# Making the second attention's keys and values during routing, and splitting them at the end of the experts

## The chip, the cores and the metric

One core of a Trainium2 chip runs the kernel; the metric is the device time of one execution in microseconds (us), the median of several. The core has five engines with a queue each: TensorE (PE in the profile; PEld is its weight load), VectorE (DVE), ScalarE (ACT), GpSimd (POOL) and SyncE (SP, which here only issues transfers; GpSimd issues the gathers). They meet at semaphores: an instruction adds to one, and another queue waits until it has a value.

## The reference

Two transformer-like layers over 2048 tokens of 256 numbers (`x`, 2 x 1024 x 256), all in fp32:

```python
x = x + tanh(g_xattn[0]) * L0_xattn(layernorm(x), ctx)   # 16 heads of 64, 154 keys per batch
x = x + tanh(g_ffn[0])   * L0_ffn(layernorm(x))          # 8 experts, top 2, silu(a) * g, width 512
x = x + tanh(g_xattn[1]) * L1_xattn(layernorm(x), ctx)   # 8 heads of 128, all 308 keys together
x = x + tanh(g_ffn[1])   * L1_ffn(layernorm(x))          # three cycles of a small coupling network
# L1_xattn: heads take batch and sequence together
kh = context @ Wk; vh = context @ Wv; qh = x @ Wq
sim = qh kh^T * 128 ** -0.5; mean = sim.mean(-1)
attn = softmax((sim - mean) * 1.5 + mean); out = (attn @ vh) @ Wout + bout
```

The keys and values of the second attention depend on the context and its weights alone, not on `x`. The mean term is folded into a shifted context, `ctx_shifted`, from which its keys are made.

## The kernel before

The program is written by hand for each engine; the order of the code is the order of each queue, and every wait is a named semaphore. Tokens lie in 16 tiles of 128. The stages follow one another:

- **First attention** (`pe_attention`, `dve_attention` and so on): 64 steps of four heads. Steps 0 to 31 use the keys `K0` and values `V` of batch 0, the rest those of batch 1. Both live in the buffer `region_a`.
- **Routing** (`pe_routing`, `dve_routing`): per tile two transposes of the normalized `x` (L1336) and a product with `Wr` (L1342) give the logits; VectorE picks two experts of each token; two products with triangles and ones (L1347, L1348, "rank") count the tokens; VectorE works out each token's slot, then 32 products (L1354, "token") invert the map. `owner` says which expert each slot tile of 128 rows belongs to.
- **Experts** (`pe_experts`, ...): 39 slot tiles. SyncE loads the expert's `W1` (1 MB) for each into a ring of three (`load_w1`, L1489), GpSimd gathers its tokens (L1640), TensorE transposes them (L1517), makes the hidden layer (L1527, `hidden`), ScalarE and VectorE make `silu(a) * g` (`gated`, L1606, into `act_sum`) and split it, and TensorE multiplies by `W2`. `b2` is read by VectorE's add of each tile's result, and VectorE's queue waits for its load (`b2_in`) ahead of the first `gated`.
- **Second attention** (`pe_pairs`, ...): two tiles (a pair) at a time, 64 steps of two heads; tile 0 and 1 need the experts' results, which GpSimd gathers by slot (L1227) and VectorE mixes into `x` (`mix`, L827, `mixed_pair`) before it normalizes them (L817). GpSimd scales each step's probabilities (L1292), TensorE transposes them (L636, `transposes`).
- **Coupling network** (`pe_coupling`, ...).

Products of the second attention are split: an operand is written as a high part rounded to fp32r (`K_high`, made by ScalarE) and the rest (`K_low`, made by VectorE or GpSimd), and three products take the place of one (L487 to L489, `pe_split`). Before the change the second attention's own keys and values are made at its start, by `pe_kv1`: four units `v` (values of 256 keys), eight `k` (keys, one per head), two `r` (values of the last 52 keys); ScalarE writes the high part straight from PSUM (`act_kv1`) and VectorE the low part (`dve_kv1`). `Wq` is split by ScalarE (L1179), VectorE (L1002) and GpSimd (L2018), and `Wo1` by ScalarE and, inside the first two steps, by GpSimd (L1297).

```python
sp.wait_ge(sem("xe_ready"), NT)                # SyncE, ahead of the experts
sp.dma_start(xn_rows..., xn_all)               # the normalized rows, 2 MB
sp.dma_start(b2[:], ...)                       # 1 MB, one row to all partitions
```

## Time and profile before

| what | value |
|---|---|
| median of 3 runs | 1012.97 us (1012.3 to 1014.51) |
| profiled execution, its own time | 1014.85 us |
| its span, first to last instruction | 1013.0 us |
| TensorE busy | 933.9 us (92%) |
| VectorE, ScalarE, GpSimd busy | 569.5, 468.2, 371.5 us |
| chain that ended last | TensorE 85%, VectorE 8%, GpSimd 2%, ScalarE 2% |
| mean granted TensorE clock | 0.952 of full |

All times below are from the start of the span of that one execution. The granted clock is given as a share of 2.4 GHz; 0.50 in a stretch is the lower level, 1.2 GHz, and a number between says for what part of the stretch each held. A wait on an engine that nobody waits for costs nothing; the chain that ended last says which work set the end.

### The profile page before, as it was taken

To read this page: it belongs to the slowest core of one execution; us is meant where nothing else is said; L and a number is where in the kernel's file an instruction comes from. 1 tells how busy PE (TensorE), PEld (TensorE's weight loads), DVE (VectorE), ACT (ScalarE), POOL (GpSimd) and SP (SyncE) were. 2 spreads that over 40 slices of the span, in tenths; PEclk is the share of its full clock that TensorE was granted. 3 is DMA by queue.
4 is the path that set the end of the run, shared out by engine and by line. 5 is a ranking of instruction groups with operands and counts; after the bars stand their busy time and mean duration, and the time that the engine had idled before them with its cause. 6 is when DMAs were issued, how large, how long until landed. Compare 5 with 4: busy or idle time off the path is not lost.

```text
span 1013.0 us, 20489 instructions
## 1 busy us (share of the span) xinstructions
PE 933.9 (92%) x6821; PEld 849.0 (84%) x6822; DVE 569.5 (56%) x1319; ACT 468.2 (46%) x1451; POOL 371.5 (37%) x498
## 2 busy tenths in 40 slices
PE   5999999999999755999999996899999999989995
PEld 3589999999998755999999974799999999975662
DVE  7554555545455464334444346777777776663273
ACT  0255555555555211444434433656555655544442
POOL 5153343433433103222222115655555643423132
PEclk9899999999999856999999998899999999999987
DMA  9400000000000044977667733100000000000002
GB/s 280 131 1 2 1 0 1 2 1 2 1 0 1 7 167 148 319 258 251 244 244 250 255 109 106 28 22 21 13 21 10 22 1 1 2 1 1 1 0 83
DMA packets 37503, 76.15 MB, mean 75 GB/s; under 512 B 5101, under 2 KB 23777, under 8 KB 37313
## 3 DMA queue, kind: packets, MB, share of 16 engines
q1 hardware_dynamic: 34033, 66.03, 19.6%
q0 software_dynamic: 3408, 9.31, 2.7%
q8 instruction: 37, 0.61, 0.3%
q14 instruction: 25, 0.20, 0.1%
HBM read 66.02 MB, written 9.31 MB: 74 GB/s over the span
## 4 chain that ended last, share of the span: by engine, by line
PE 85%; DVE 8%; POOL 2%; ACT 2%; issue 1%; DMA 1%; POOLq 0%; DVEq 0%; SPq 0%; ACTq 0%
PE banks L1527 14%; PE banks L487 11%; PE banks L489 11%; PE banks L488 11%; PE banks L521 8%; PE banks L495 6%; PE banks L506 6%; PE banks L513 3%; PE banks L636 3%; PE banks L1738 2%; PE banks L353 1%; PE banks L1342 1%; PE banks L1742 1%; PE banks L1517 1%; PE banks L1724 1%
## 5 line engine op out<-in xcount | busy, mean ns | idle before, releaser
L1527 PE MATMUL banks<-region_b,region_a 128*128 128x128 f32 x1248 | 147.8, 277 | 1.1 <-ACT region_b L1560 0.5
L1527 PEld LDWEIGHTS banks<-region_b,region_a 128*128 128x128 f32 x1248 | 144.6, 194 | 1.8 <-issue 0.9
L1102 ACT ACTIVATE region_a<-banks,negmax 128x154 f32<-128x154 f32 x256 | 96.0, 388 | 91.0 <-DVE negmax L851 89.8
L1257 POOL TENSOR_TENSOR region_a<-region_a,recip 128x512 f32<-128x512 f32 x64 | 66.5, 1039 | 178.7 <-DVE recip L857 178.7
L1292 POOL TENSOR_TENSOR region_a<-region_a,recip 128x640 f32<-128x640 f32 x64 | 80.2, 1253 | 107.7 <-DVE recip L971 107.5
L1606 DVE SCALAR_TENSOR_TENSOR region_a<-banks,region_b,region_a 128x128 f32<-128x128 f32 x156 | 43.9, 345 | 108.9 <-PE banks L1527 108.9
L521 PE MATMUL banks<-region_a 128*128 128x128 f32 x768 | 96.6, 275 | 1.9 <-DVE oT_low L874 1.8
L521 PEld LDWEIGHTS banks<-region_a 128*128 128x128 f32 x768 | 91.0, 192 | 2.9 <-issue 2.2
L495 PE MATMUL banks<-region_a 128*128 128x308 f32 x256 | 77.1, 425 | 0.0
L487 PE MATMUL banks<-Wo_high,oT_high 128*128 128x256 f32 x256 | 76.0, 297 | 0.9 <-DVE oT_low L874 0.9
L1161 ACT CAST pT_high<-banks 128x640 fp32r<-128x640 f32 x64 | 44.4, 694 | 66.8 <-PE banks L636 66.8
L1567 ACT ACTIVATE region_a<-banks,region_b 128x128 f32<-128x128 f32 x156 | 44.5, 368 | 62.5 <-PE banks L1527 62.5
L1172 ACT ACTIVATE region_a<-banks,negmax 128x308 f32<-128x308 f32 x128 | 65.2, 516 | 17.1 <-DVE negmax L966 16.2
L489 PE MATMUL banks<-Wo_high,oT_low 128*128 128x256 f32 x256 | 72.2, 282 | 0.0
L488 PE MATMUL banks<-Wo_low,oT_high 128*128 128x256 f32 x256 | 72.0, 281 | 0.0
L506 PE MATMUL banks<-xT,region_b 128*128 128x128 f32 x512 | 66.0, 285 | 1.2 <-ACT region_a L1088 0.7
L506 PEld LDWEIGHTS banks<-xT,region_b 128*128 128x128 f32 x512 | 62.9, 201 | 1.9 <-ACT region_a L1088 1.0
L874 DVE TENSOR_TENSOR oT_low<-banks,oT_high 128x256 fp32r<-128x256 f32 x64 | 27.2, 425 | 60.8 <-ACT oT_high L1094 60.8
L976 DVE TENSOR_TENSOR pT_low<-banks,pT_high 128x640 fp32r<-128x640 f32 x64 | 52.7, 823 | 15.0 <-ACT pT_high L1161 13.9
L851 DVE TENSOR_REDUCE negmax<-banks 128x4 f32<-128x616 f32 x64 | 51.0, 797 | 15.5 <-PE banks L495 15.3
L966 DVE TENSOR_REDUCE negmax<-banks 128x2 f32<-128x616 f32 x64 | 50.5, 789 | 14.0 <-PE banks L489 12.5
L487 PE MATMUL banks<-pT_high,V_high 128*128 128x256 f32 x192 | 54.5, 284 | 1.8 <-DVE oT_low L982 1.8
(249 smaller groups left out, 2470.0 us busy)
## 6 DMA issues: line engine op xcount, KB each, us to landing
region_a<-in_L_ffn_W SPq DMA_DIRECT2D x39, 1024.0 KB
y_slots<-region_b SPq DMA_DIRECT2D x39, 128.0 KB
W<-in_L_ffn_W SPq DMA_DIRECT2D x1, 4096.0 KB, 17.4
region_b<-in_L_xattn_Wq SPq DMA_DIRECT2D x2, 1024.0 KB
xn_rows<-region_b SPq DMA_DIRECT2D x1, 2048.0 KB, 8.5
out<-x SPq DMA_DIRECT2D x4, 512.0 KB, 2.9
region_b<-in_L_xattn_Wk SPq DMA_DIRECT2D x2, 768.0 KB, 7.3
region_b<-in_L_xattn_Wv SPq DMA_DIRECT2D x2, 768.0 KB
```

What stands on the lines that cost most here:

```text
L487: pe.matmul(o, left[0], right[0], start=start, stop=False)
L488: pe.matmul(o, left[0], right[1], start=False, stop=False)
L489: return pe.matmul(o, left[1], right[0], start=False, stop=stop)
L495: mm = pe.matmul(o, q[:, r, c, :], K0[:, b, c, :], start=True, stop=True)
L506: mm = pe.matmul(misc_ps[:, c * P:(c + 1) * P], Wq[:, k, (4 * half + c) * P:(4 * half + c + 1) * P], xT[:, r, k, :], start=(k == 0), stop= ...
L521: mm = pe.matmul(o_ps[:, u * P:(u + 1) * P], V[:, b, 2 * g + u, i, :], probsT[:, g % 2, m * P:(m + 1) * P], start=(i == 0), stop=(i == 2))
L976: dve.tensor_tensor(pT_low[:, n // 2 % 2, :, at], probsT_ps[:, 0:640].rearrange("p (m n) -> p m n", m=5), pT_high[:, n // 2 % 2, :, at].bi ...
L1102: e = act.activation(pr[:, j, 0:L.keys], scores[:, g % 2, u, i * L.keys:(i + 1) * L.keys], ACT.Exp, bias=negmax[:, g % 2, j:j + 1], accum_ ...
L1172: e = act.activation(probs1[:, n % 2, u, 12 * u:12 * u + KEYS], scores[:, n % 2, u, 0:KEYS], ACT.Exp, bias=negmax[:, n % 2, u:u + 1], accu ...
L1257: pool.tensor_tensor(whole, pr[:, :, 0:split], rc.broadcast_to([P, L.hs, split]), ALU.mult)
L1292: pool.tensor_tensor(probs1[:, n % 2], probs1[:, n % 2], rc, ALU.mult).then_inc(sem("p_norm"), 1)
L1527: mm = pe.matmul(banks[:, 2 * r + part, m * P:(m + 1) * P], W1[:, r, k, cols], xgT[:, r, k, :], start=(k == 0), stop=(k == DK - 1))
```

## The change

- The context shift moves into the first attention: VectorE makes `ctx_sum` and `ctx_shifted` in tile 9, and SyncE loads `Wk`, `Wv` of the second layer once step 31 has been done, into `region_a` where batch 0's keys lay.
- The fourteen units are made in routing: two `v` ahead of the tiles' transposes, eight `k` and two `v` between the rank and the token products, two `r` behind the token products. ScalarE only copies them to plain fp32 buffers `V1`, `K1`.
- `Wq1` and `Wo1` are loaded ahead of the experts. `W1`'s ring is kept, but two of its three places lie where `Wk1`, `Wv1` and `ctx_shifted` are: the first load of slot tiles 1 and 2, and that of `b2` between them, wait until all units are made (`kv1_ps`).
- `Wq1` is split in four parts in slot tiles 33 to 36, by ScalarE (high) and GpSimd (low). Keys, values and `Wo1` are split in six parts (`L1_PARTS`) from the end of the experts on, by ScalarE and VectorE from SBUF. `mixed_pair(2)` stands behind the first `row_max`.
- `a_act` and `act_sum` lose their ring of three; `gated` waits for the `act_low` of the tile before. The logits use two banks in turn in place of four.

```diff
+        KV1_UNITS = [("v", 0, 0), ("v", 0, 1)] + [("k", c, 0) for c in range(NC)] + [("v", 1, 0), ("v", 1, 1)] + \
+            [("r", 0, half) for half in range(2)]
+        KV1_BANKS = (6, 7) + 2 * (0, 1, 2, 3) + (7, 0) + (4, 5)
+        KV1_FREE = (0, 0) + (0, 0, 0, 0, 3, 4, 5, 6) + (2, 7) + (0, 0)
+        KV1_AFTER_RANK, KV1_AFTER_TOKENS = 2, 12
...
-            pe_kv1(pe, "vk")
             pe.wait_ge(sem("xn_ready"), t0 + 2)
             pe_pair_x(pe)
-            pe_kv1(pe, "r")
-            pe.wait_ge(sem("Wq_split"), 2)
+            pe.wait_ge(sem("query_low"), QUERY_PARTS)
             pe.wait_ge(sem("xt2_sb"), 1)
             pe_pair_q(pe, 0)
-            pe.wait_ge(sem("kv1_sb"), KV1_BEFORE_R + 2)
+            pe.wait_ge(sem("l1_low"), 2)
             pe.wait_ge(sem("q2_sb"), 1)
             pe_pair_scores(pe, 0)
             pe_pair_q(pe, 1)
+            pe.wait_ge(sem("l1_low"), 4)
...
+                        if is_body(t, NT // 2 + 1) and g == 1:
+                            dve.wait_ge(sem("o_ps"), STEPS // 2)
+                            dve.tensor_reduce(ctx_sum, ctxT[:, :, :], AX.X, ALU.add).then_inc(sem("ctx_sum"), 1)
+                        if is_body(t, NT // 2 + 1) and g == 2:
+                            dve.wait_ge(sem("ctx_sum"), 1)
+                            rest = KEYS - 2 * P
+                            for to, at, keys in ((0, 2 * P, rest), (rest, 0, KEYS)):
...
-            dve.wait_ge(sem("ey_sb"), SLOTS)
-            dve.tensor_reduce(ctx_sum, ctxT[:, :, :], AX.X, ALU.add).then_inc(sem("ctx_sum"), 1)
-            dve.wait_ge(sem("ctx_sum"), 1)
-            for at, keys in ((0, KEYS), (KEYS, 2 * P)):
...
-            last.then_inc(sem("ctx_shifted"), 1)
-            dve_kv1(dve, L1, "v")
-            dve_kv1(dve, L1, "k", range(0, 4))
+            def part_low(n):
+                raw, high, low, c = L1_PARTS[n]
+                dve.wait_ge(sem("l1_high"), n + 1)
+                dve.tensor_tensor(low[:, c:c + 4], raw[:, c:c + 4], high[:, c:c + 4].bitcast(F32), ALU.subtract)                    .then_inc(sem("l1_low"), 1)
+
+            for n in range(4):
+                part_low(n)
             mixed_pair(0)
-            dve_kv1(dve, L1, "k", range(4, NC))
+            part_low(4)
             dve.wait_ge(sem("rstd_in"), 3)
             dve_normalize(dve, 0, xn)
             dve_normalize(dve, 1, xn_odd)
             pair_x_rest(1)
-            dve.wait_ge(sem("Wq_high"), 1)
-            dve.tensor_tensor(Wq_low[:, 1], Wq[:, 1], Wq_high[:, 1].bitcast(F32), ALU.subtract)\
-                .then_inc(sem("Wq_split"), 1)
-            dve_kv1(dve, L1, "r")
-            mixed_pair(2)
+            part_low(5)
             pair_q_rest(1, 0)
             row_max(0, 0)
+            mixed_pair(2)
             pair_q_rest(2, 1)
...
+        L1_PARTS = [(K1, K_high, K_low, 0), (K1, K_high, K_low, 4), (V1, V_high, V_low, 0), (V1, V_high, V_low, 4),
+                    (Wo1, Wo_high, Wo_low, 0), (Wo1, Wo_high, Wo_low, 4)]
...
-            act_kv1(act, L1, "v")
-            act_kv1(act, L1, "k", range(0, 4))
-            act.wait_ge(sem("wq_in"), 32)
-            act.copy(Wq_high[:], Wq[:]).then_inc(sem("Wq_high"), 1)
-            act_kv1(act, L1, "k", range(4, NC))
+            act.wait_ge(sem("ey_ps"), SLOTS)
+            for raw, high, low, c in L1_PARTS:
+                act.copy(high[:, c:c + 4], raw[:, c:c + 4]).then_inc(sem("l1_high"), 1)
             x_high(1)
-            act_kv1(act, L1, "r")
             pair_q_high(1, 0)
             act.wait_ge(sem("pads_zero"), 2)
             exponentials(0, 0)
             pair_q_high(2, 1)
-            act.wait_ge(sem("wo_in"), 32)
-            act.copy(Wo_high[:], Wo1).then_inc(sem("Wo_high"), 1)
...
-                    if first and n in (1, 2):
-
-                        pool.wait_ge(sem("Wo_high"), 2)
-                        part = slice((n - 1) * NC // 2, n * NC // 2)
-                        pool.tensor_tensor(Wo_low[:, part], Wo1[:, part], Wo_high[:, part].bitcast(F32),
-                                           ALU.subtract).then_inc(sem("Wo1_split"), 1)
...
             pe.wait_ge(sem("y_done"), NT)
...
+            pe_kv1(pe, (0, 1))
+            pe.wait_ge(sem("b1_ready"), 1)
...
+            pe_kv1(pe, range(KV1_AFTER_RANK, KV1_AFTER_TOKENS))
+            pe.wait_ge(sem("kv1_raw"), KV1_AFTER_RANK)
...
+            pe_kv1(pe, range(KV1_AFTER_TOKENS, len(KV1_UNITS)))
...
+            pool.memset(V1[:, :, 2, :], 0.0).then_inc(sem("v_zero"), 1)
...
+            act_kv1(act, (0, 1))
...
+            act_kv1(act, range(KV1_AFTER_RANK, KV1_AFTER_TOKENS))
             act.wait_ge(sem("margin_ready"), 1)
             act.activation(weight[:, 1, :], weight[:, 0, :], ACT.Exp).then_inc(sem("margin_exp"), 1)
             act.activation(table[:, 0:1], zero_eps[:, 0:1], ACT.Silu)
+            act_kv1(act, range(KV1_AFTER_TOKENS, len(KV1_UNITS)))
...
             sp.wait_ge(sem("owner_ready"), 1)
-            for j in range(RING):
-                load_w1(j, j)
+            load_w1(0, 0)
+            sp.wait_ge(sem("kv1_ps"), len(KV1_UNITS))
+            load_w1(1, 1)
+            sp.dma_start(b2[:], t_in["L0_ffn_b2"].rearrange("e n -> (e n)").partition_broadcast(P)
+                         .rearrange("p (e n) -> p e n", e=E)).then_inc(sem("b2_in"), 16)
+            load_w1(2, 2)
             sp.wait_ge(sem("hg_ps"), 1)
             load_w1(RING, 0)
...
-                    if isinstance(j, int) and j == 0:
-                        sp.wait_ge(sem("xn_stored"), 16)
-                        load_keys_values(sp, 1)
...
+            pe.wait_ge(sem("kv1_raw"), len(KV1_UNITS) - 2)
             turn_x(0, 0)
             pe.wait_ge(sem("xgt_sb"), 1)
             hidden(0, 0)
             turn_x(1, 0)
             pe.wait_ge(sem("W2_split"), NT)
+            pe.wait_ge(sem("kv1_raw"), len(KV1_UNITS))
 
...
+            def query_high(n):
+
+                act.copy(Wq_high_parts[:, n], Wq1_parts[:, n]).then_inc(sem("query_high"), 1)
...
+                    if query_part(j) is not None:
+                        query_high(query_part(j))
...
+                if not (isinstance(j, int) and j == 0):
+                    dve.wait_ge(sem("act_low"), j)
...
+                    if query_part(j) is not None:
+                        n = query_part(j)
+                        pool.wait_ge(sem("query_high"), n + 1)
+                        pool.tensor_tensor(Wq_low_parts[:, n], Wq1_parts[:, n], Wq_high_parts[:, n].bitcast(F32),
+                                           ALU.subtract).then_inc(sem("query_low"), 1)
...
+            sp.wait_ge(sem("o_ps"), STEPS // 2)
+            load_keys_values(sp, 1)
             sp.wait_ge(sem("xe_ready"), NT)
             sp.dma_start(xn_rows.rearrange("(t p) d -> p t d", p=P), xn_all).then_inc(sem("xn_stored"), 16)
-            sp.dma_start(b2[:], t_in["L0_ffn_b2"].rearrange("e n -> (e n)").partition_broadcast(P)
-                         .rearrange("p (e n) -> p e n", e=E)).then_inc(sem("b2_in"), 16)
+            load_attention(sp, 1)
             sp_experts(sp)
 
             for r in range(RING):
                 sp.wait_ge(sem(f"ey_out{r}"), 16 * (SLOTS // RING))
-            load_attention(sp, 1)
+            load_bias(sp, 1)
             sp.wait_ge(sem("mixed"), 4)
             load_coupling(sp)
             outs = out.rearrange("b s d -> (b s) d").rearrange("(t p) d -> p t d", p=P)
...
-            pool.memset(V_high[:, :, 2, :].bitcast(F32), 0.0)
-            pool.memset(V_low[:, :, 2, :].bitcast(F32), 0.0).then_inc(sem("v_zero"), 1)
             for r in range(RING):
                 pool.wait_ge(sem(f"ey_out{r}"), 16 * (SLOTS // RING))
             for t in range(5):
                 if t == 2:
-                    pool.wait_ge(sem("Wq_high"), 1)
-                    pool.tensor_tensor(Wq_low[:, 0], Wq[:, 0], Wq_high[:, 0].bitcast(F32), ALU.subtract)\
-                        .then_inc(sem("Wq_split"), 1)
                     pool_rstd(pool, 0, 2, "in", 3)
```

TensorE from the rank products (L1347, L1348) to the first expert tile (L1517), before:

```order
L1347 MATMUL banks<-either,before 128x128 [waits before_ready,either_ready]
L1348 MATMUL banks<-either,ones 128x128
L1354 MATMUL banks<-region_b 128x39 [waits in_row_ready,numbered_ready]
L1354 MATMUL banks<-region_b 128x39 x7
L1354 MATMUL banks<-region_b 128x39 [waits in_row_ready,numbered_ready]
L1354 MATMUL banks<-region_b 128x39 x7
L1354 MATMUL banks<-region_b 128x39 [waits in_row_ready,numbered_ready]
L1354 MATMUL banks<-region_b 128x39 x7
L1354 MATMUL banks<-region_b 128x39 [waits in_row_ready,numbered_ready]
L1354 MATMUL banks<-region_b 128x39 x7
L1517 MATMUL banks<-ident,region_b 128x128 [waits xg_in0,token_ready,owner_ready]
L1517 MATMUL banks<-ident,region_b 128x128
```


The same place in the changed kernel (rank products L1330, L1331; L427 makes keys), first rows:

```order
L1330 MATMUL banks<-either,before 128x128 [waits before_ready,either_ready]
L1331 MATMUL banks<-either,ones 128x128
L427 MATMUL banks<-region_a 128x308 [waits ctx_shifted]
L427 MATMUL banks<-region_a 128x308 x7
L427 MATMUL banks<-region_a 128x308 [waits kv1_raw]
L427 MATMUL banks<-region_a 128x308
```


and its last rows there (L431 makes values, `ctx_rem` marks the `r` units; L1339 are the token products):

```order
L431 MATMUL banks<-region_a,ctxT 128x512 [waits kv1_raw]
L431 MATMUL banks<-region_a,ctxT 128x512
L1339 MATMUL banks<-region_b 128x39 [waits in_row_ready,numbered_ready,kv1_raw]
L1339 MATMUL banks<-region_b 128x39 x7
L1339 MATMUL banks<-region_b 128x39 [waits in_row_ready,numbered_ready]
L1339 MATMUL banks<-region_b 128x39 x7
L1339 MATMUL banks<-region_b 128x39 [waits in_row_ready,numbered_ready]
L1339 MATMUL banks<-region_b 128x39 x7
L1339 MATMUL banks<-region_b 128x39 [waits in_row_ready,numbered_ready]
L1339 MATMUL banks<-region_b 128x39 x7
L431 MATMUL banks<-region_a,ctx_rem 128x512 x4
L1517 MATMUL banks<-ident,region_b 128x128 [waits kv1_raw,xg_in0,token_ready,owner_ready]
```


The token products now stand behind twelve units and the first expert transpose behind two more. SyncE from the store of `xn_rows` to the second load of `W1`, before (the `in_L_ffn_b` row is `b2`, `TENSOR_LOAD owner` reads a tile's expert):

```order
L1965 DMA xn_rows<-region_b 128x16x256 [waits xe_ready]
L1966 DMA region_a<-in_L_ffn_b 128x2048
L1477 TENSOR_LOAD owner [waits owner_ready]
L1477 ISA x2
L1489 ISA
L1489 DMA region_a<-in_L_ffn_W 128x2x1024
L1477 TENSOR_LOAD owner
L1477 ISA x2
L1489 ISA
L1489 DMA region_a<-in_L_ffn_W 128x2x1024
```


and of the changed kernel, from the first load of `W1` to the third:

```order
L1488 DMA region_a<-in_L_ffn_W 128x2x1024
L1476 TENSOR_LOAD owner [waits kv1_ps]
L1476 ISA x2
L1488 ISA
L1488 DMA region_a<-in_L_ffn_W 128x2x1024
L1494 DMA region_a<-in_L_ffn_b 128x2048
L1476 TENSOR_LOAD owner
L1476 ISA x2
L1488 ISA
L1488 DMA region_a<-in_L_ffn_W 128x2x1024
```


`b2` has moved from ahead of the first `W1` load to between the second and the third, behind the wait for `kv1_ps`. VectorE at the start of the second attention, from the split of `Wq` to the second split of `q`, before:

```order
L1002 TENSOR_TENSOR Wq_low<-region_b,Wq_high 128x1024 [waits Wq_high]
L463 TENSOR_TENSOR V_low<-banks,V_high 64x2x128 [waits v_zero,kv1_high]
L463 TENSOR_TENSOR V_low<-banks,V_high 64x2x128
L463 TENSOR_TENSOR V_low<-banks,V_high 64x2x128 [waits v_zero,kv1_high]
L463 TENSOR_TENSOR V_low<-banks,V_high 64x2x128
L827 SCALAR_TENSOR_TENSOR x<-W,weight,x 128x256 [waits gathered0]
L827 SCALAR_TENSOR_TENSOR x<-W,weight,x 128x256 [waits mixed_first]
L827 SCALAR_TENSOR_TENSOR x<-W,weight,x 128x256 [waits gathered1]
L827 SCALAR_TENSOR_TENSOR x<-W,weight,x 128x256 [waits mixed_first]
L783 BN_STATS stats<-x 128x6 [waits mixed] x2
L789 BN_AGGR mean_var<-stats 128x2 [waits stats_in] x2
L956 TENSOR_TENSOR q_low<-banks,q_high 128x512 [waits q2_high]
```


and of the changed kernel, from the last part of `Wo1` to the same split:

```order
L982 TENSOR_TENSOR Wo_low<-region_a,Wo_high 128x1024 [waits l1_high]
L950 TENSOR_TENSOR q_low<-banks,q_high 128x512 [waits q2_high]
L960 TENSOR_REDUCE negmax<-banks 128x2 [waits s_ps]
L809 SCALAR_TENSOR_TENSOR x<-W,weight,x 128x256 [waits gathered0]
L809 SCALAR_TENSOR_TENSOR x<-W,weight,x 128x256 [waits mixed_first]
L809 SCALAR_TENSOR_TENSOR x<-W,weight,x 128x256 [waits gathered1]
L809 SCALAR_TENSOR_TENSOR x<-W,weight,x 128x256 [waits mixed_first]
L765 BN_STATS stats<-x 128x6 [waits mixed] x2
L771 BN_AGGR mean_var<-stats 128x2 [waits stats_in] x2
L950 TENSOR_TENSOR q_low<-banks,q_high 128x512 [waits q2_high]
```


The mixing of tiles 2 and 3 (the four rows on `gathered0`, `gathered1`) stood ahead of the first `q_low`; now it stands behind the first `q_low` and the first row maximum, and only the second `q_low` is behind it.

## Rows read from the trace of the kernel before

**Rows 1.** Stages of the span: busy time by engine, clock, DMA share, GB/s.

```profile
60.00:325.00 265.00, 264.66 (x2039) 244.87 (x2038) 140.37 (x302) 146.80 (x638) 99.38 (x157) 1.00 0.00 1
...
400.00:450.00 50.00, 49.96 (x441) 49.78 (x440) 20.05 (x55) 20.45 (x59) 10.45 (x19) 1.00 0.87 285
...
640.00:660.00 20.00, 15.58 (x109) 14.58 (x108) 16.60 (x29) 11.07 (x30) 16.00 (x14) 0.91 0.07 20
```

**Rows 2.** Chain that ended last, routing to the first experts (start, us, what).

```profile
345.44 0.48 DVE x L928
...
348.37 1.88 PE banks L1336 x8
...
364.33 3.23 PE banks L1342 x16
...
370.47 0.44 PE banks L1348 x2
...
378.89 7.27 DVE region_b L1436 x32
...
388.11 3.02 DMA region_b<-xn_rows,token_now
...
392.45 5.66 PE banks L1527 x32
...
404.29 3.57 PE banks L1527 x32
```

**Rows 3.** Stretches of two us, columns as in rows 1.

```profile
348.00:350.00 2.00, 1.63 (x8) 1.50 (x9) 2.00 (x7) 0.89 (x3) 0.00 (x0) 0.63 0.00 0
...
396.00:398.00 2.00, 2.00 (x19) 2.00 (x18) 0.00 (x0) 1.14 (x4) 0.00 (x0) 0.93 0.00 0
```

**Rows 4.** SyncE's issues, and one us of the transfers they start.

```profile
353.60 1.96 SPq L1966 DMA_DIRECT2D region_a<-in_L_ffn_b  x1
...
375.18 0.39 SPq L1489 DMA_DIRECT2D region_a<-in_L_ffn_W  x1
...
378.00:379.00 1.00, 0.00 (x0) 0.00 (x0) 1.00 (x3) 0.00 (x0) 0.03 (x1) 0.50 1.01 418
```

**Rows 5.** TensorE's timeline from the last expert tile.

```profile
600.46 7.03 PE L422 MATMUL banks<-region_b,ctxT 96*128 96x512 f32 x16
...
607.33 8.46 PE L418 MATMUL banks<-W,region_b 96*128 96x308 f32 x32
...
621.20 5.49 PE L422 MATMUL banks<-region_b,ctx_rem 96*128 96x512 f32 x8
...
639.83 0.71 PE L636 MATMUL banks<-ident,region_a 128*128 128x128 f32 x5
...
648.25 0.77 PE L636 MATMUL banks<-ident,region_a 128*128 128x128 f32 x5 [3.61 <-POOL region_a L1292]
```

**Rows 6.** Same chain as rows 2, between the experts and the second attention.

```profile
608.16 6.02 DMA W<-y_slots,slot_now
...
614.21 2.40 DVE x L827
...
619.91 0.33 DVE region_a L817
...
634.22 0.21 PE banks L488
```

**Rows 7.** GpSimd's, ScalarE's and VectorE's timelines there.

```profile
612.00 1.89 ACT L1179 CAST Wq_high<-region_b 128x2048 fp32r<-128x2048 f32 x1
...
613.97 2.34 POOL L2018 TENSOR_TENSOR Wq_low<-region_b,Wq_high 128x1024 fp32r<-128x1024 f32 x1 [3.68 <-ACT Wq_high L1179]
...
622.66 1.22 DVE L1002 TENSOR_TENSOR Wq_low<-region_b,Wq_high 128x1024 fp32r<-128x1024 f32 x1
```

**Rows 8.** VectorE's timeline in the first attention and in the experts.

```profile
309.69 0.18 DVE L857 RECIPROCAL recip<-sums 128x4 f32<-128x4 f32 x1 [1.19 <-ACT region_a L1102]
...
408.10 1.13 DVE L1606 SCALAR_TENSOR_TENSOR region_a<-banks,region_b,region_a 128x128 f32<-128x128 f32 x4 [2.62 <-PE banks L1527]
```

215 lines of the change are left out of this document (104 added, 111 removed).

## The prediction

> **What bounds the kernel now.** I read the stages first. In the first attention TensorE is busy 264.66 of 265 us and in the experts 49.96 of 50, both at full clock [rows 1]; what shortens another engine there shortens nothing. The chain of waits says where TensorE is not the bound: from the end of the first attention to the first expert tiles the chain runs through VectorE's slot arithmetic, a gather and products at the lower clock [rows 2], and between the experts and the second attention through a store, gathers, mixing and GpSimd [rows 6]. In those two places TensorE has holes: none of its work lies between the rank products' end at 370.9 and the last of 32 compares at 386.16 but the small token products [rows 2]; and it idles 3.61 us before 648.25 [rows 5]. The units that the change moves take 7.03 us for four `v`, 8.46 for eight `k`, and 5.49 for two `r` [rows 5]: 1.76, 1.06 and 2.7 each, the last mostly at the lower clock. The `v` and `k` units lie where TensorE waits for the gathers anyhow; the `r` units, the last splits and the late gathers are on the path.
>
> **The change part by part.** Everything is against the profiled span of 1013.0. The profiled execution took 1014.85, the median is 1012.97; I subtract the sum from the median.
>
> *First attention.* VectorE gets a sum and two shifts over 96x616, some 2.2 us over two steps. It idles 1.19 us before a step's reciprocals [rows 8], so about that much fits twice. I take +0.4; bounds 0 and +1.5 (nearly all of it on the path). Loading 1.5 MB in a stage with a DMA share of 0.00 [rows 1] costs nothing.
>
> *Logits.* The chain reached the transposes at 348.37, after the last `x` was done at 345.92 [rows 2]. Two `v` units, 3.5 us from 346.2, end at 349.7: +1.35, and ScalarE's copy of the second adds 0.3. Against that stands the clock. In 348 to 350 it was 0.63 on average, so it fell at about 348.5 [rows 3], 3.1 us after the dense products ended near 345.4. With dense work until 349.7 I expect the fall near 352.8. Sixteen tiles took 19.2 us at the lower level (348.37 to 367.56 [rows 2]), so 3.1 us at the higher do the work of 6.2: -3.1. Sum -1.45; bounds +1.65 (clock falls at once) and -1.8.
>
> *Between rank and tokens.* Eight `k` and two `v` units are 12.0 us at full clock. The clock rises only under dense work: the first hidden layer began at 392.45 and the mean of 396 to 398 is 0.93, a rise near 396.3, 3.8 us later [rows 2, 3]. That adds 1.9: 13.9 us, where the last compare comes 15.25 us after the rank products. The cover is VectorE's compares; the slack is 1.3 us. Cost 0. If the clock never rose there it would be 24 us: +8.8.
>
> *First expert tiles.* Two `r` units (3.5 us) run behind the token products, from 386.7 to 390.3, while tile 0's gather lands, at 391.13 as before (388.11 and 3.02 [rows 2]). TensorE then meets that tile at the higher clock: the hidden layer takes 3.57 as at 404.29 in place of 5.66 [rows 2], the transposes 0.45 less; it ends near 395.6. But `W1` of tile 1, `b2` and `W1` of tile 2 now wait for all units. Before, the first load left at 375.18 and there was ample time [rows 4]. One MB takes 2.5 us at the 418 GB/s that these loads reached [rows 4]; with 1.0 to read the owner and issue and 1.4 to the first byte (chosen; an issue alone is 0.39, a whole gather 3.0), tile 1's weights land at 395.2, `b2` (issue 1.96 [rows 4], hidden behind the transfer) at 397.8, tile 2's at 400.3. VectorE's first `gated` waits for `b2`; its work, ScalarE's high part and VectorE's low part take 2.6, so tile 0's last product runs 400.4 to 401.9 and the third hidden layer starts at 401.9 instead of 404.29: -2.4. Bounds: at the 285 GB/s of the expert stage [rows 1] it starts at about 404.1, and with another us of latency it is +0.8; -2.9 if `b2` is early. A `gated` that comes late delays the `act_low` behind it and TensorE's last product of that tile, nothing else.
>
> *Steady experts.* The new wait of `gated` on the `act_low` of the tile before is for work that ended before VectorE's 2.62 us of idle time [rows 8]: 0. The query parts: GpSimd needs 2.34 for 1024 columns [rows 7], so 1.2 for each of four; I take +0.2, bounds 0 and +1.
>
> *To the first step of the second attention.* Removed from this place: 2 MB of loads that ran against the gathers (the last gather was issued at 608.16 and landed after 6.02 [rows 6], where the expert's gather took 3.02 [rows 2]); GpSimd's part of `Wq`; the `r` units. Added: six splits from SBUF. ScalarE casts 2048 columns in 1.89, VectorE subtracts 1024 in 1.22 [rows 7]; the first four parts (5536 columns) take VectorE some 6.4 us behind ScalarE, 601.9 to 608.3, under the gathers, which now land near 611.2. Mixing tile 1, statistics and GpSimd's two steps end at 614.2.
>
> Here a row and a rule meet. A mix of 128x256 that takes 0.48 elsewhere (the same operation [rows 2]) took 2.40 from 614.21, while GpSimd ran `Wq_low` from 613.97 to 616.31 [rows 6, 7]. The Trainium skill, SBUF — State Buffer, "Who interferes with whom", says a VectorE instruction with two SBUF inputs and a GpSimd instruction that reads SBUF exclude each other, whoever starts first. By that rule the change is hit too: VectorE's `part_low(4)` would hold up GpSimd's rstd, +1.2; by the row, which shows only the other order, between 0 and that. I take +0.7 from the length of the part. (With 0 the sum below would be -15.95, with the rule's 1.2 it would be -14.75.)
>
> So the normalizing ends at 615.6 instead of 620.24 [rows 6]: 4.6 earlier. Then transposes 1.1, high and low part of `x` 1.4, twelve products at 0.21 [rows 6] 2.6, parts of `q` 1.4, scores 1.5, maximum and exponentials 2: 625.8. GpSimd is next: tile 4's gather waits until tile 2 is mixed (625.6), takes 2.8, then the bias and rstd 1.8, then the first scaling 1.25: TensorE's first step's transposes at 631.8 instead of 639.83 [rows 5]: -8.0. Bounds -5.5 and -10.
>
> *First pair.* `Wo_low`'s two halves leave GpSimd's queue (shape and length as `Wq_low`, 2.34). They made TensorE idle 3.61 [rows 5], and a mean clock of 0.91 over 640 to 660 [rows 1] means 3.6 us at the lower level, 1.8 lost: 5.4 in all. I take -4 of it, as the pair's own chain of scores, maximum, exponential, scaling may show through; bounds 0 and -5.4.
>
> **Sum**: +0.4 - 1.45 + 0 - 2.4 + 0.2 - 8.0 - 4.0 = -15.25. 1012.97 - 15.25 = **997.7 us**.
>
> **Rivals.** *The first pair is bound by its own chain* once the splits are gone: the last term is 0, 1001.7. For it: VectorE is busy 16.60 of 20 us and GpSimd 16.00 there [rows 1]; against it: both lose work. *The gathers land late all the same*, since 6.02 may be their own small pieces and not the loads: the normalizing gains 2 instead of 4.6, 1000.3. Against it: the 3.02 of the expert's gather. *The clock stays low over the key products*: tokens +8.8, the `r` units take 7 instead of 3.5 and the loads wait for them, so the third hidden layer starts at 414.1, +9.8 in place of -2.4: 1009.9. Against it: units of the same kind ran at the higher level after the experts [rows 5]. *The clock stays up over the logits*: sixteen tiles at half of 19.2 save 8 instead of 1.45: 991.2. Against it: it fell while the transposes of 348.37 ran [rows 3]. The Trainium skill, TensorE: Matmul & The Clock Gate, "PE-mode transpose", says that transposes don't count as busy in the same way; the trace agrees as far as that row goes. *The experts' tile gets longer*, the case that ends slower: with one `act_sum`, `gated`, ScalarE's high part and `act_low` follow each other; if that or the order of `a_act` used up the 2.62 of idle time and 0.4 more, 39 tiles would eat the gain; at 0.6 a tile, 23.4 - 15.25, it is 1021. Against it: nothing in the chain is longer than before.
>
> **How the numbers follow.** Chances: forecast 0.52, own range 993 to 1002; pair's own chain 0.2; late gathers 0.12; clock up over the logits 0.07; clock low over the keys 0.06; longer expert tiles 0.03. The range 992 to 1004.5 leaves out the two last, most of the 991 case, and part of the tails of the bounds. A measurement of this kernel tells about 0.2% from no change (2 us). All cases but the slow tile lie below that; for causes that I don't see I leave 0.03 within 0.2% and 0.04 slower.
>
> **What would show it.** In the profile after: the logits' last product 1 to 2 us earlier; token products ending where VectorE's compares end; the first hidden layer near 3.6; a wait for `b2` of under 2 us on VectorE, and the third hidden layer some 14 us after the first gather's issue; expert tiles at an unchanged pace; the last of the first four gathers landed 3 us after its issue; the first L636 transposes some 31 us after the last expert product instead of 39; no idle stretch of 3 us in the first pair. A clock of 0.5 through the key products, or a stall of several us on `w1_in` or `b2_in`, would make it wrong.

## The result, and the profile after

The changed kernel took 999.91 us (median of 4 runs, 998.48 to 1004.79) against 1013.01 us (1012.3 to 1014.51): a ratio of 0.9877 with a 95% interval of 0.9842 to 0.9913. The profiled execution took 1000.18, its span is 998.4 us, 14.6 below the span before. The forecast was 997.7, range 992 to 1004.5. Run again later, the same kernel gave 997.84 to 1007.67 (6 runs); the median of all ten is 1001.7. Why it scatters more than the kernel before is part of what follows.

TensorE's timeline through routing and the first expert tiles (start, us, engine, line, operation, tiles, count, idle before it and what ended that):

```profile
345.02 0.28 PE L472 MATMUL banks<-Wo_high,oT_low 128*128 128x256 f32 x1
...
358.28 3.16 PE L1325 MATMUL banks<-Wr,region_b 128*128 128x8 f32 x16
...
364.15 0.64 PE L1331 MATMUL banks<-either,ones 128*128 128x128 f32 x2
364.58 10.55 PE L427 MATMUL banks<-region_a 96*128 96x308 f32 x32
...
380.20 0.36 PE L1339 MATMUL banks<-region_b 128*128 128x39 f16 x8 [0.95 <-DVE region_b L1423]
```

```profile
385.95 3.84 PE L1527 MATMUL banks<-region_b,region_a 128*128 128x128 f32 x32 [0.52 <-ACT region_b L1562]
...
390.70 3.81 PE L1527 MATMUL banks<-region_b,region_a 128*128 128x128 f32 x32 [0.69 <-DMA region_a<-in_L_ffn_W]
...
397.17 0.38 PE L470 MATMUL banks<-W_high,actT_high 128*128 x1 [2.44 <-DVE actT_low L1624]
...
398.70 3.74 PE L1527 MATMUL banks<-region_b,region_a 128*128 128x128 f32 x32
```

The rank products (L1331) end at 364.79, where rows 2 have 370.9: 6.1 earlier. The last token products end at 380.56, before at 386.73 (first row of the fence on the kernel before, below): 6.2 earlier. But the third hidden layer starts at 398.70 (398.86 in the chain that ended last) and not 404.29 [rows 2, the chain], which is 5.4 earlier: 0.7 was given back between the token products and there. In front of tile 0's last product (L470) TensorE idled 2.44 us.

The granted clock, in stretches of 2 us (engines' busy times, clock, DMA share, GB/s; compare [rows 3]):

```profile
348.00:350.00 2.00, 2.00 (x9) 0.99 (x8) 2.00 (x5) 0.77 (x2) 0.66 (x1) 1.00 0.00 0
356.00:358.00 2.00, 2.00 (x21) 2.00 (x21) 1.60 (x16) 1.23 (x4) 0.00 (x0) 1.00 1.04 347
358.00:360.00 2.00, 2.00 (x14) 2.00 (x14) 1.66 (x16) 0.60 (x2) 0.00 (x0) 0.64 1.03 325
366.00:368.00 2.00, 2.00 (x5) 1.35 (x4) 1.79 (x7) 0.43 (x1) 0.00 (x0) 0.50 0.62 218
368.00:370.00 2.00, 2.00 (x7) 1.35 (x6) 1.79 (x8) 0.44 (x2) 0.00 (x0) 0.80 0.00 0
```

It was still full at 358 and fell near 358.6 (0.64 on average over 358 to 360), 13.3 us after the first attention's last product (345.30) and 8.8 after the `v` units' end (349.8), where I expected the fall at 352.8. Under the key products (from 364.58) it rose near 368.8, 4.2 us after their start, close to the 3.8 expected.

GpSimd's and VectorE's timelines between the experts and the second attention, and TensorE's transposes of probabilities (L619) of the first, third and seventh step:

```profile
598.13 1.84 POOL L1213 DMA_INDIRECT W<-y_slots,slot_now  x1 [0.33 <-POOL slot_now L1208]
600.27 1.32 POOL L1213 DMA_INDIRECT W<-y_slots,slot_now  x1 [0.31 <-issue]
601.59 0.90 POOL L1208 COPY slot_now<-slot 128x2 uint32<-128x2 uint32 x1
602.76 0.97 POOL L1213 DMA_INDIRECT W<-y_slots,slot_now  x1 [0.27 <-POOL slot_now L1208]
604.03 1.16 POOL L1213 DMA_INDIRECT W<-y_slots,slot_now  x1 [0.30 <-issue]
...
609.01 1.09 POOL L780 TENSOR_TENSOR mean_var<-mean_var,zero_eps 128x4 f32<-128x4 f32 x1 [2.64 <-DVE mean_var L771]
```

```profile
595.11 0.42 DVE L1638 TENSOR_TENSOR region_b<-banks,region_a 128x256 f32<-128x256 f32 x1 [1.99 <-PE banks L472]
596.31 2.79 DVE L982 TENSOR_TENSOR K_low<-region_a,K_high 128x1232 fp32r<-128x1232 f32 x2 [0.77 <-ACT K_high L1169]
599.02 3.42 DVE L982 TENSOR_TENSOR V_low<-region_a,V_high 128x1536 fp32r<-128x1536 f32 x2
...
606.98 1.00 DVE L809 SCALAR_TENSOR_TENSOR x<-W,weight,x 128x256 f32<-128x256 f32 x2 [2.60 <-DMA W<-y_slots,slot_now]
...
608.84 1.19 DVE L982 TENSOR_TENSOR Wo_low<-region_a,Wo_high 128x1024 fp32r<-128x1024 f32 x1
610.93 0.41 DVE L799 TENSOR_SCALAR xn<-x,mean_var,rstd 128x256 f32<-128x256 f32 x1 [0.90 <-POOL rstd L783]
```

```profile
628.27 0.77 PE L619 MATMUL banks<-ident,region_a 128*128 128x128 f32 x5 [0.90 <-POOL region_a L1278]
...
634.67 0.77 PE L619 MATMUL banks<-ident,region_a 128*128 128x128 f32 x5 [1.42 <-POOL region_a L1278]
...
646.95 0.76 PE L619 MATMUL banks<-ident,region_a 128*128 128x128 f32 x5
```

The marks of the kernel before that the rows ahead of the forecast don't show: its last token products, its last add of the experts, its transposes (L636) of the seventh step:

```profile
386.30 0.43 PE L1354 MATMUL banks<-region_b 128*128 128x39 f16 x8 [0.87 <-DVE region_b L1436]
```

```profile
600.79 0.43 DVE L1627 TENSOR_TENSOR region_b<-banks,region_a 128x256 f32<-128x256 f32 x1 [1.99 <-PE banks L489]
```

```profile
662.04 0.76 PE L636 MATMUL banks<-ident,region_a 128*128 128x128 f32 x5
```

From the start of the last add (L1638, 595.11; before, 600.79) to the first L619 it is 33.16 us; before, 600.79 to 639.83 [rows 5], 39.04. From there to the seventh step's 18.68; before, 22.21. The fourth gather landed 2.92 us after its issue at 604.03, not 6.02 [rows 6]. But the four issues took 1.84, 1.32, 0.97 and 1.16 us, and the slot copy between them 0.90. TensorE idles 1.42 us before the third step, where it was 3.61 [rows 5].

### The profile page after: what moved, and what is told of

Read it like the earlier page. It is cut to its first block, busy times and chain, and to the rows that moved or that the text cites. A ratio compares the mean times of both kernels' runs of the same rounds, so it can differ in the third digit from the quotient of the medians.

```text
span 998.4 us, 20489 instructions
## 1 busy us (share of the span) xinstructions
PE 925.4 (93%) x6821; PEld 839.2 (84%) x6822; DVE 563.0 (56%) x1308; ACT 473.3 (47%) x1459; POOL 372.3 (37%) x498
## 4 chain that ended last, share of the span: by engine, by line
PE 85%; DVE 7%; POOL 2%; DMA 2%; ACT 2%; issue 2%; POOLq 0%; DVEq 0%; SPq 0%; ACTq 0%
PE banks L1527 14%; PE banks L470 11%; PE banks L472 11%; PE banks L471 11%; PE banks L504 9%; PE banks L478 7%; PE banks L489 6%; PE banks L496 3%; PE banks L619 3%; PE banks L1754 2%; PE banks L375 1%; PE banks L1758 1%; POOL W L1213 1%; DVE region_a L2060 1%; PE banks L1762 1%
## 5 line engine op out<-in xcount | busy, mean ns | idle before, releaser
L1527 PE MATMUL banks<-region_b,region_a 128*128 128x128 f32 x1248 | 145.9, 275 | 1.2 <-DMA region_a<-in_L_ffn_W 0.7
L1527 PEld LDWEIGHTS banks<-region_b,region_a 128*128 128x128 f32 x1248 | 142.8, 192 | 1.7 <-issue 0.9
L1617 DVE SCALAR_TENSOR_TENSOR region_b<-banks,region_a,region_b 128x128 f32<-128x128 f32 x156 | 43.9, 344 | 109.7 <-PE banks L1527 109.0
L470 PE MATMUL banks<-Wo_high,oT_high 128*128 128x256 f32 x256 | 75.8, 296 | 0.9 <-DVE oT_low L856 0.9
L1569 ACT ACTIVATE region_b<-banks,region_a 128x128 f32<-128x128 f32 x156 | 44.5, 368 | 57.1 <-PE banks L1527 57.1
L833 DVE TENSOR_REDUCE negmax<-banks 128x4 f32<-128x616 f32 x64 | 51.0, 796 | 15.4 <-PE banks L478 15.2
L470 PE MATMUL banks<-pT_high,V_high 128*128 128x256 f32 x192 | 54.8, 285 | 1.8 <-DVE oT_low L976 1.8
## 6 DMA issues: line engine op xcount, KB each, us to landing
region_b<-in_L_xattn_Wq SPq DMA_DIRECT2D x1, 1024.0 KB, 11.3
```

Of the source, the lines that this page charges most:

```text
L470: pe.matmul(o, left[0], right[0], start=start, stop=False)
L1527: mm = pe.matmul(banks[:, 2 * r + part, m * P:(m + 1) * P], W1[r][:, k, cols], xgT[:, r, k, :], start=(k == 0), stop=(k == DK - 1))
```

## Experiments

All are edits of the changed kernel. Where stages are compared, each is measured from a mark of its own run, since the prologue shifts them: the first attention's last product ends anywhere from 342.6 to 347.2. Medians, and ratios to the kernel before in runs on the same chip:

| kernel | median, us | lowest to highest, runs | ratio, 95% interval |
|---|---|---|---|
| `v_behind_rank` | 1009.78 | 1005.48 to 1014.26, 10 | 0.9966, 0.9948 to 0.9983 |
| `gap_half` | 1008.31 | 1005.58 to 1009.42, 8 | 0.9943, 0.9921 to 0.9965 |
| `gap_filled` | 1002.73 | 1000.52 to 1008.09, 4 | 0.9893, 0.9854 to 0.9932 |
| `b2_at_first_add` | 997.34 | 996.56 to 1004.19, 4 | 0.9854, 0.9815 to 0.9893 |
| `w1_one_early` | 998.46 | 994.29 to 1003.5, 4 | 0.9863, 0.982 to 0.9907 |
| `splits_behind_mix` | 1002.69 | 1001.13 to 1006.55, 5 | 0.9876, 0.9857 to 0.9895 |
| `splits_spread` | 997.8 | 996.54 to 1005.2, 4 | 0.986, 0.9815 to 0.9906 |
| `loads_back` | 1002.08 | 997.84 to 1002.83, 4 | 0.9869, 0.9839 to 0.9899 |
| `wo_on_gpsimd` | 1003.05 | 1001.31 to 1004.41, 4 | 0.9895, 0.987 to 0.9919 |
| `after_again` | 1005.39 | 997.84 to 1007.67, 6 | 0.9886, 0.9842 to 0.993 |
| `combined` | 997.05 | 995.51 to 999.92, 6 | 0.9828, 0.9796 to 0.9861 |

With such scatter the times alone tell only the clear cases apart; the verdicts rest on the traces.

### What carried the clock over the logits

`v_behind_rank` moves the two `v` units; `gap_filled` and `gap_half` put transposes of the identity, whose result nobody reads, in their place:

```diff
             pe.transpose(banks[:, 5, 0:E * 2 * HK], b1_rows, ...).then_inc(sem("b1_ps"), 1)
-            pe_kv1(pe, (0, 1))
+            for n in range(18):      # gap_filled 18, gap_half 9, v_behind_rank none
+                pe.transpose(banks[:, 6, 0:P], ident[:], ident[:])
...
-            pe_kv1(pe, range(KV1_AFTER_RANK, KV1_AFTER_TOKENS))   # the same on ScalarE
+            pe_kv1(pe, range(0, KV1_AFTER_TOKENS))
```

> The two v units go from in front of the routing transposes to behind the rank products, with the ten others. Theory A, those units carried the clock over the logits: without them the granted clock falls near 348.5 us again as in the kernel before, a tile takes 1.2 us instead of 0.62, the rank products end near 370.8 instead of 364.80, and twelve units (16 us, and 2 more while the clock is still low) end near 388, 2 us behind VectorE's last compare: 6 + 2 = 8 us longer than the changed kernel, about 1008. Rival, the clock has another reason (the earlier layout, the later start of the transposes): it stays up to about 358 all the same, rank products end near 363, and only the units behind them cost something: 0 to 3 us.

> As v_behind_rank, but TensorE turns the identity 18 times (128x128, result unused, about 2.3 us) in the place of the two units, so that it doesn't stand still between the first attention's last product and the first routing transposes. Theory A, the clock was carried by products of 512 columns: it falls near 349, as without the units; rank products end near 371, in all 8 us longer than the changed kernel. Rival B, the hole of 2 us in TensorE's work was what brought the clock down: it stays up to 355 or longer, rank products end at 363 to 366, and the time is 0 to 3 us above the changed kernel's.

> As gap_filled with 9 transposes of the identity instead of 18, so that TensorE stands still for about 1.8 us, instead of 0.7 with 18 and 2.8 with none, between its last product of the first attention and the routing transposes. If the length of the hole alone decides, and it decides somewhere between 0.7 and 2.1 us: either the clock falls 3 to 4 us behind the attention's end and the rank products end 25.3 us after it, or it stays up for 12 to 13 us and they end 19.6 us after it. A value between the two would speak for a graded reason: the amount of work of all kinds.

One-us stretches of `v_behind_rank`, `gap_filled` and, run again unaltered, of the changed kernel (`after_again`) in which the clock fell:

```profile
346.00:347.00 1.00, 0.72 (x5) 0.57 (x6) 1.00 (x4) 0.27 (x2) 0.00 (x0) 0.94 0.00 0
347.00:348.00 1.00, 1.00 (x6) 0.95 (x6) 1.00 (x5) 0.78 (x4) 0.00 (x0) 0.50 0.00 0
```

```profile
357.00:358.00 1.00, 1.00 (x9) 1.00 (x9) 0.79 (x9) 0.54 (x2) 0.00 (x0) 0.72 1.02 318
```

```profile
355.00:356.00 1.00, 1.00 (x12) 1.00 (x11) 0.97 (x7) 0.58 (x2) 0.00 (x0) 0.91 0.00 0
```

A mean of 0.94 over a us that ends at 0.50 means a fall after 0.88 of it: 346.88. So read, and with the ends of the last dense product and of the rank products from the timelines ("dense" are the closely packed products of 256 columns that end the first attention; each row but the last is one execution):

| kernel | between the dense products and the logits | clock fell, us after the dense end | rank products' end, us after it |
|---|---|---|---|
| before | hole of 2.1 us | 3.1 | 25.5 |
| `v_behind_rank` | hole of 2.8 us | 4.3 | 26.0 |
| `gap_half` | 9 transposes, hole of 1.7 us | 9.6 | 22.1 |
| `gap_filled` | 18 transposes, hole of 0.7 us | 13.2 | 19.5 |
| after | two `v` units, no hole | 13.3 | 19.5 |
| `after_again` | the same | 8.6 | 23.7 |
| seven below | the same | 8.5 to 16.6 | 18.2 to 23.8 |

Two things follow. The units did not act by their 512 columns: 2.2 us of transposes in their place did as well (19.5 us for both, one execution each), so theory A is wrong on that and rival B is right. With nothing there the clock fell after 3.1 and 4.3 us. Whether it is the hole's length or TensorE's share of work up to there can't be told apart by these runs, since each transpose adds to one and takes from the other. `gap_half` came out between, and its single profile lies within what the same instructions scatter, but the times say more. That profile (1005.58) is of the fastest of its eight executions, and the one of `v_behind_rank` (1005.48) of the fastest of ten. With all twelve units behind the rank products the way from there to the last token products is longer too: 17.1 us in `v_behind_rank`, 18.0 in `gap_filled`, 18.3 in `gap_half`, against 15.8. Less what that adds, the medians stand 6.7, -1.2 and 4.1 us above the 1001.7 of the changed kernel. By this estimate 18 transposes buy back all that the missing units cost, and 9 less than half. (The 8.1 us in all of `v_behind_rank` are the amount that theory A gave.) And the moment of the fall is no property of the kernel: nine executions whose TensorE ran the same instructions up to there fell between 8.5 and 16.6 us after the dense products, with rank products 18.2 to 23.8 us after them (mean 20.8). The changed kernel's profiled run (19.5) was a lucky one; on average the place gives 25.5 - 20.8 = 4.7 us, not 6 (against the one profile of the kernel before). This is also most of the scatter: `after_again`, profiled at a span of 1005.9, was 4.2 us later here than the first profile, and its prologue 1.9 us longer.

### What held up the first expert tiles

`b2_at_first_add` moves one wait; `w1_one_early` also lets tile 1's `W1` lie over `Wk` alone and loads it behind the key products:

```diff
-            dve.wait_ge(sem("b2_in"), 16)                # dve_experts, at the start
...
+                    if isinstance(j, int) and j == 0:
+                        dve.wait_ge(sem("b2_in"), 16)    # ahead of the add that reads b2
# w1_one_early, sp_experts
+            sp.wait_ge(sem("kv1_ps"), 10)
+            load_w1(1, 1)
             sp.wait_ge(sem("kv1_ps"), len(KV1_UNITS))
-            load_w1(1, 1)
+            load_w1(2, 2)
             sp.dma_start(b2[:], ...)
-            load_w1(2, 2)
```

> VectorE's wait for b2 goes from ahead of the first gated to ahead of the first y add, which is the first to read it; the loads stay where they are. If b2 holds the first gated: gated of tile 0 starts by 390 instead of 394.52, its last product begins when the second hidden layer ends (394.5) instead of at 397.17, the third hidden layer starts at 396.2 instead of 398.86, and the kernel is 2.5 us faster, 997.4. Rival, VectorE was held by something else, or the third tile's weights (W1) are as late: the third hidden layer starts at 398 or later, and the time changes by under 1 us.

> As b2_at_first_add, and the places of W1 in region_a are exchanged so that tile 1's lies over Wk only: it is loaded when the key products have ended (near 375) instead of behind the r units (384.1); tile 2's and then b2 follow the r units. Theory: what is left of the loads' delay is W1 of tile 1: its wait of 0.69 on TensorE goes and the second hidden layer starts about 0.7 us earlier than in b2_at_first_add; the third starts 15.0 us after the token products instead of 15.8; 996.6. Rival: tile 2's W1 or b2 is late next, and the third hidden layer starts no earlier.

In the changed kernel: SyncE's issue of `b2`, the times from issue to landing of tile 1's `W1` and of `b2` (least and most), and VectorE's queue as it reads `owner` for its first `gated`:

```profile
385.27 0.47 SPq L1494 DMA_DIRECT2D region_a<-in_L_ffn_b  x1
```

```profile
DMA to landing us min/median/max: 5.6/6.8/8.0
```

```profile
L1476 DVEq TENSOR_LOAD <-owner x1: 553/553/553, 393.4 to 393.4; - x1
```

`b2` landed at 393.3, 8.0 us after its issue. Only then could VectorE's queue read the tile's expert from `owner`, which `gated` does behind the wait, and `gated` began at 394.52, 1.2 us later.

VectorE's first `gated` (L1616) and TensorE's hidden layers (L1527) in `b2_at_first_add`:

```profile
388.77 1.13 DVE L1616 SCALAR_TENSOR_TENSOR region_b<-banks,region_a,region_b 128x128 f32<-128x128 f32 x4 [8.45 <-PE banks L1527]
```

```profile
378.87 0.36 PE L1339 MATMUL banks<-region_b 128*128 128x39 f16 x8 [0.42 <-DVE region_b L1423]
...
394.99 3.81 PE L1527 MATMUL banks<-region_b,region_a 128*128 128x128 f32 x32
```

`gated` now runs as soon as the first hidden layer is done, the third hidden layer starts 15.8 us after the last token products (379.23) instead of 18.1 to 18.3, and the fourth 21.1 instead of 23.5 after: 2.4 us, as expected. With `W1` of tile 1 early as well, TensorE still idles 0.69 before the second hidden layer, now for ScalarE's copy of the turned `x`, and the third starts after 15.5. So the theory's 0.7 was wrong and the rival's outcome right, 0.3 more at most, though not for the rival's reason: in the changed kernel the copy ended at 390.42 and `W1` landed at 390.44, so that the load by itself delayed nothing. In time the two are no different (997.34 and 998.46). Only these two kernels and `combined` are free of the idle time before tile 0's last product, and none of their profiles shows the second fall of the clock that five of the others show at its end (last section).

### The splits, the gathers and the port

`splits_behind_mix` puts `part_low(0)` to `part_low(3)` behind `mixed_pair(0)`. `splits_spread` lays them out: 

```diff
-            for n in range(4):
-                part_low(n)
+            part_low(0)
+            dve.wait_ge(sem("four_issued"), 1)   # GpSimd, behind its fourth gather
+            part_low(1)
             mixed_pair(0)
-            part_low(4)
             dve.wait_ge(sem("rstd_in"), 3)
             dve_normalize(dve, 0, xn)
             dve_normalize(dve, 1, xn_odd)
+            part_low(2)                          # L1_PARTS: K, K, Wo, Wo, V, V
             pair_x_rest(1)
-            part_low(5)
+            part_low(3)
+            part_low(4)
             pair_q_rest(1, 0)
+            part_low(5)
             row_max(0, 0)
```

> VectorE's first four low parts go behind the mixing of tiles 0 and 1, so that no VectorE work runs while GpSimd issues the four gathers; ScalarE's casts still do. Theory, VectorE's subtractions lengthen GpSimd's issues: they take 0.95 to 1.05 each again (1.84, 1.32, 0.97, 1.16 in the changed kernel), the slot copy 0.2 instead of 0.90, and the last of the four is issued near 602.0 instead of 604.03 and lands near 605. Rival, ScalarE's casts or a first use do it: 1.84 and 1.32 stay. The time: mixing ends near 606, then 7.4 us of splits stand in front of the normalizing, which starts near 613.5 instead of 610.9, so 2 to 3 us slower, 1002 to 1003.

> The changed kernel with VectorE's low parts laid out of GpSimd's way: one K part under the y store, the second behind the issue of the four gathers, the other four in VectorE's holes behind the normalizing. Theory (VectorE's subtractions on SBUF hold up GpSimd's issues and its rstd): the last of the four gathers is issued 2 us earlier, mean_var and rstd take 0.20 and 0.73 instead of 1.09 and 0.73, the normalizing starts 13 us after the last expert product instead of 16.1, and the kernel is 2.5 to 3 us faster, near 997. Rival, the moved parts hold up the gathers of tiles 2 and 3 instead, and the first scaling waits for them: under 1 us gained, and the holes before the first L619 transposes grow by what the normalizing won.

GpSimd's timeline in `splits_behind_mix`, where VectorE is idle under the gathers and subtracts (L982) from 610.51 to 617.7:

```profile
601.83 0.99 POOL L1212 DMA_INDIRECT W<-y_slots,slot_now  x1 [0.53 <-POOL slot_now L1207]
603.12 0.95 POOL L1212 DMA_INDIRECT W<-y_slots,slot_now  x1 [0.30 <-issue]
...
605.81 0.95 POOL L1212 DMA_INDIRECT W<-y_slots,slot_now  x1 [0.30 <-issue]
...
610.68 1.30 POOL L780 TENSOR_TENSOR mean_var<-mean_var,zero_eps 128x4 f32<-128x4 f32 x1 [2.74 <-DVE mean_var L771]
612.06 1.80 POOL L783 TENSOR_TENSOR rstd<-mean_var,minus_half 128x2 f32<-128x2 f32 x1
613.84 1.15 POOL L1207 COPY slot_now<-slot 128x2 uint32<-128x2 uint32 x1
615.27 2.26 POOL L1212 DMA_INDIRECT W<-y_slots,slot_now  x1 [0.29 <-POOL slot_now L1207]
```

ScalarE cast K, V and Wo from 598.69 to 605.7 there, and the issues still took 0.99, 0.95, 0.97 and 0.95. So VectorE's subtractions are the cause: behind the mix they hold up what GpSimd then does, `mean_var` 1.30 instead of 0.20, `rstd` 1.80 instead of 0.73, a copy 1.15, a gather's issue 2.26. The normalizing came 18.85 us after the last add, and the median is 1002.69, both near what was expected. In `splits_spread` it is from the start of the last add to the normalizing 13.45 us instead of 15.82, and to the first L619 30.8 instead of 33.2 (32.7 to 32.9 in the six other runs that have the changed kernel's order there). So 2.0 to 2.4 are kept, although one issue for tile 3 took 2.47.

The Trainium skill, SBUF — State Buffer, "Who interferes with whom", has both: VectorE with two SBUF inputs shuts out a GpSimd instruction that reads SBUF, and a gather that seems slowed by VectorE was held up in making its descriptors. The rows above agree with both sentences. They don't agree with a third one there, that `tensor_tensor` did not stall a DMA: VectorE's subtractions are `tensor_tensor`, and a gather's issue beside them took 1.84 and 2.26 us instead of 0.95.

`loads_back` loads the 2 MB again, into space that nobody reads, where the kernel before loaded them; `wo_on_gpsimd` gives `Wo_low` back to GpSimd:

```diff
# loads_back, SyncE behind the last y stores
+            sp.dma_start(dead[:, 0:2048], ... Wq ...)
+            sp.dma_start(dead[:, 2048:4096], ... Wout ...)
             load_bias(sp, 1)
# wo_on_gpsimd, pool_pairs; part_low(4) and part_low(5) are gone from VectorE
+                    if first and n in (1, 2):
+                        pool.wait_ge(sem("l1_high"), 4 + n)
+                        part = slice(4 * (n - 1), 4 * n)
+                        pool.tensor_tensor(Wo_low[:, part], Wo1[:, part], Wo_high[:, part]..., ALU.subtract)
```

> The changed kernel, and SyncE loads Wq and Wout of the second layer once more (2 MB, into free space of region_b, read by nobody) at the place where the kernel before loaded them, behind the last y store. Theory of the prediction (those loads made the gathers late): the fourth gather lands 5 to 6 us after its issue instead of 2.92, the normalizing starts 2.5 to 3 us later, and the kernel is about 3 us slower, 1003. Rival (the gathers are late by their own small pieces, or were in the kernel before for another reason): it lands within 3.5 us, and nothing changes.

> The changed kernel with Wo_low's two parts back in GpSimd's queue, behind the second and third scaling of the first pair, as before the change. Theory of the prediction (these two made TensorE's idle 3.61 us and the low clock of the first pair): TensorE idles some 3.5 us again before the transposes of step 3, and the kernel loses 4 (3 to 5.4), less 0.9 that rstd wins since VectorE's part no longer runs beside it: 1003 plus or minus 1. Rival (the pair is bound by its own chain of scores, maximum, exponentials, scaling): 0 to 1 us slower.

VectorE's mixing in `loads_back`; GpSimd and TensorE in the first pair of `wo_on_gpsimd`:

```profile
597.60 0.42 DVE L1640 TENSOR_TENSOR region_b<-banks,region_a 128x256 f32<-128x256 f32 x1 [1.99 <-PE banks L473]
...
609.07 1.92 DVE L810 SCALAR_TENSOR_TENSOR x<-W,weight,x 128x256 f32<-128x256 f32 x4 [4.15 <-DMA W<-y_slots,slot_now]
...
613.95 0.41 DVE L800 TENSOR_SCALAR xn<-x,mean_var,rstd 128x256 f32<-128x256 f32 x1 [0.90 <-POOL rstd L784]
```

```profile
608.04 0.20 POOL L780 TENSOR_TENSOR mean_var<-mean_var,zero_eps 128x4 f32<-128x4 f32 x1 [2.65 <-DVE mean_var L771]
...
631.52 2.36 POOL L1286 TENSOR_TENSOR Wo_low<-region_a,Wo_high 128x1024 fp32r<-128x1024 f32 x1
```

```profile
635.14 0.77 PE L619 MATMUL banks<-ident,region_a 128*128 128x128 f32 x5 [3.73 <-POOL region_a L1276]
```

`loads_back`: VectorE's mixing of tile 0 waited for its second gather (issued at 602.75) until 609.07, 6.3 us, when the loads ended (they kept the DMA full until 608.9); but the fourth, issued at 606.51, landed 3.4 us later, in time for the mixing to run through. The normalizing came 16.35 us after the last add instead of 15.82: the loads cost 0.5, not 3. The two costs overlap: what the subtractions add to the issues is time in which the loads get done. So neither theory as I put it: the loads do make gathers late (the rival's 3.5 us held for the fourth, but the first took 6.6 and the second 6.3), and yet were worth little here. How much they would cost beside `splits_spread` no run shows. By estimate it is about 2 us: its mixing starts 9.5 us after the last add, and the loads end 11.3 after it.

`wo_on_gpsimd`: TensorE idles 3.73 us before the third step again; from the normalizing to the sixth step's L619 it is 35.9 us instead of 32.5, 3.4 more, and `mean_var` is back at 0.20 (normalizing 0.8 earlier). The median, 1003.05, is the 1003 expected. The first pair was bound by GpSimd's queue, as forecast.

### All together

`combined` is `w1_one_early` and `splits_spread`, and on GpSimd:

```diff
+                if t == 4:
+                    gate_bias(pool, 1)           # from pool_pairs into the idle time before tile 4
...
+                    if first and n == 0:
+                        pool_rstd(pool, 2, 2, "in", 4)   # behind the first scaling, not ahead
```

> w1_one_early and splits_spread together, and in GpSimd's queue the bias goes into its idle time before tile 4's slots and the first scaling ahead of the second rstd. If the gains are of different places and add: 2.8 from the loads, 2.4 from the splits, 1.4 from the bias and rstd (0.62, 0.20, 0.73) that no longer stand before the first scaling: 6.6 less than the changed kernel, 993.3. Rival: TensorE's first step then waits for VectorE's q_low behind tile 4's mixing (L809 waits 2.6 for its gather), so the scaling's 1.4 is lost: 994.7.

> The changed kernel unaltered, as the measure for the other two on the same chip: 999 to 1001.

```profile
616.33 0.62 POOL L1228 TENSOR_TENSOR gated_bo<-gated_bo,gates 128x256 f32<-128x256 f32 x1
...
623.39 1.26 POOL L1281 TENSOR_TENSOR region_a<-region_a,recip 128x640 f32<-128x640 f32 x1
```

```profile
622.82 0.58 PE L470 MATMUL banks<-xT_high,Wq_high 128*128 128x256 f32 x1 [2.26 <-DVE q_low L950]
...
626.66 0.71 PE L619 MATMUL banks<-ident,region_a 128*128 128x128 f32 x5
```

It is the fastest kernel of all by its median, 997.05, with all six runs below the 1001.7 of the changed kernel's ten; but its interval and that of `after_again` overlap by a little (0.9861 against 0.9842). Its own places agree with the parts: third hidden layer 15.4 us after the token products (384.14 to 399.54), first L619 30.7 after the last add (595.95). The early scaling (623.39, in `splits_spread` 625.36) won nothing there: TensorE came to its transposes behind products that had waited 2.26 us for an earlier `q_low`, until 622.82. The rival was right in amount, and nearly in its reason. The forecast 993.3 was missed by 3.8 us: 1.4 for the scaling that won nothing, and 1.8 since I took the gains from 999.91, the median of the first four executions, and not from the 1001.7 of ten; 0.6 stay open. In its profiled execution the clock fell 8.5 us after the dense products, 4.3 us dearer in the logits than in the profile I added to.

## Why the prediction came out as it did

The sum of the profiled execution, each term by the marks above, against the forecast:

| step | forecast | measured |
|---|---|---|
| first attention | +0.4 | 0 |
| logits | -1.45 | -6.1 (-4.7 on the average of nine) |
| between rank and tokens | 0 | 0 (15.77 us, before 15.83) |
| first expert tiles | -2.4 | +0.7 |
| steady experts | +0.2 | -0.2 |
| to the first L619 | -8.0 | -5.9 |
| first pair | -4.0 | -3.5 |
| after it | 0 | +0.5 |
| sum | -15.25 | -14.6 (rounded terms) |

- **First attention.** In 60 to 325 VectorE is busy 141.95 us instead of 140.37 [rows 1], TensorE 264.66 as before: VectorE's idle time took the sum and the shifts.
- **Logits.** Mis-sized, and for a wrong reason. I carried the 3.1 us between the last dense product and the fall over from the kernel before and let it start anew at 349.7. But there TensorE had also stood still for 2.1 us; without that hole the clock held 8.5 to 16.6 us (whether for want of the hole or for the work in its place stays open). The rival "the clock stays up over the logits" (0.07, a gain of 8) came closer than the forecast in the profiled execution; on the average, 4.7, both are 3.3 off. The Trainium skill, TensorE: Matmul & The Clock Gate, "PE-mode transpose", which I counted against it, speaks for the other outcome; the trace doesn't agree as far as `gap_filled` goes, where 18 transposes held the clock as well as the `v` units (a fall after 13.2 us against 13.3, one execution each).
- **Between rank and tokens.** Right: the rise came 4.2 us after the start, the products ended at 378.6 before the last compare at 380.07.
- **First expert tiles.** The step that failed, by the size of its terms and by one that it left out. I had tile 1's `W1` land 4.9 us behind the last `r` unit, `b2` 2.6 behind that, and tile 0's last product start 10.1 behind the units; it started 13.1 behind. Of the 3.0 more, 1.4 are `W1`'s: it came 6.3 behind the units (384.10 to 390.44), 5.6 of it from issue to landing, where I had 3.9 (1.4 to the first byte and 2.5 at 418 GB/s); the loads moved 121 GB/s in 384 to 386, 262 in 386 to 388 and 426 only from 388 on, and the same load alone, tile 0's at 370, took 4.9. `b2` came 2.9 behind `W1` instead of 2.6: 0.3. The other 1.2 I had put at nothing: behind its wait for `b2` VectorE's queue still reads `owner` before it can start `gated`. The order of waits was as written, and `b2_at_first_add` shows what of it was needless: 2.4 us for a wait that stood three steps too early (tile 0's `gated` and `act_low` and tile 1's `gated`, ahead of the add that reads `b2`). "A wait for `b2` of under 2 us" was the sign that I had named, and it was 3.5 (the first hidden layer's end at 389.79 to 393.3).
- **Steady experts, query parts.** Right: a tile takes 5.22 us as before.
- **To the first step.** -4.6 was forecast up to the normalizing; it was -2.9. The gathers landed 2.9 us after the last issue, as forecast, but the last issue itself came 8.92 us after the last add's start instead of 7.37 (608.16 [rows 6] less 600.79). I weighed the shared port for `rstd` alone (forecast +0.7, measured 0.9) and laid 6.4 us of the same subtractions beside the gathers at no cost; they cost 1.6, and `splits_spread` takes 2.4 back with both. That the missing loads earn 3 us is not borne out: `loads_back` puts them at 0.5 with the subtractions in place. From the normalizing to the first step it was -3.0 instead of the forecast's -3.4. My sum has a slip there: its terms from 615.6 on make 625.6 and 631.45 and not 625.8 and 631.8, which would have given -8.4.
- **First pair.** Right, in place and size: `wo_on_gpsimd` gives 3.4 back.

So the total was right by luck, by two errors of opposite sign: 4.65 too little for the logits, 5.2 too much for the expert tiles and the way to the first step. The logits' gain was itself a good draw of the clock: with its average the sum would be -13.2. (The listed chances add to 1.00 already, without the 0.07 left for causes that I didn't see.)

## What to carry to other kernels

Look at what stands behind a waiting instruction in every queue before calling its wait free: one semaphore waited for three steps too early cost 2.4 us here, 1.2 of it a read of the tile's expert that stood behind it, and the idle time it made was followed by a fall of the clock in five of seven executions. Work moved "under" another engine's transfers has a price if both engines read SBUF: check VectorE's two-input instructions against GpSimd's issues, and put them where GpSimd is idle. And take a clock's fall in one profile as one draw: compare several executions before a term rests on it.

## What the runs showed of the hardware

- The granted clock fell at times that differ by 8 us between executions of the same instructions (8.5 to 16.6 us after the last dense product), and this alone moves the kernel by up to 5.6 us (rank products 18.2 to 23.8 us after it).
- In seven of the thirteen profiled executions the clock fell once more between 380 and 407 (in `loads_back` twice). Five of these eight falls came within 0.5 us of the end of TensorE's idle time before tile 0's last product, which the wait for `b2` makes (2.4 to 2.8 us there): in `wo_on_gpsimd`, at 394.34, the third hidden layer then started 19.6 us after the token products instead of 18.1. Two more executions idled as long (2.44 and 2.92) and kept the clock; the three without that wait had no such fall. So the wait may cost 1.5 us now and then on top of its 2.4. The other three falls came ahead of it, under the token products and `r` units (`loads_back`, at 380.9) and the first hidden layer (`splits_spread`, at 386.0, and `v_behind_rank`), which took 5.46 us instead of 3.84. What brings them about is open.
- GpSimd's gather issue is 0.94 to 1.09 us alone and up to 2.47 beside VectorE's subtractions on SBUF; ScalarE's casts beside it cost nothing (0.95 to 0.99 in `splits_behind_mix`).
